# Third cross attention: five of the sixteen heads shifted by their maximum on GpSimd

## The reference

```python
scores = jnp.einsum('blhe,bshe->bhls', q, k)          # 16 heads, 77 keys
causal = jnp.triu(jnp.ones((l, s), bool), k=1)
scores = jnp.where(causal[None, None], -jnp.inf, scores)
A = jax.nn.softmax(scale * scores, axis=-1)
out = jnp.einsum('bhls,bshd->blhd', A, v).reshape(b, l, H * DV)
return out @ Wo + bo
```

## Time and profile before

| | us |
|---|---|
| median of 3 runs | 1044.64 (1040.2 to 1047.47) |
| profiled execution | 1049.98 |
| its span | 1047.8 |

### The profile page before, as it was taken

The page is one execution under the profiler, slowest core; times in us unless marked ns, Lnnn a source line. Parts: engine busy times, 40 slices in busy tenths (PEclk is TensorE's granted clock), DMA queues, the critical chain, the costliest instruction groups (busy, mean ns, idle before and its releaser), DMA issues.

```text
span 1047.8 us, 19571 instructions
## 1 busy us (share of the span) xinstructions
PE 920.8 (88%) x6337; PEld 658.4 (63%) x6337; DVE 778.0 (74%) x2080; ACT 557.4 (53%) x1494; POOL 495.5 (47%) x467
## 2 busy tenths in 40 slices
PE   6999895898778999779987698988989999989987
PEld 4787633777678999647774243434437677668873
DVE  5989998999767877779995576776734644589982
ACT  3775556896445555624442166666754233445533
POOL 5444554676066664535556667574530600024430
PEclk8999896999789999879999579999999999999998
DMA  9300000000111111500000322221002000000001
GB/s 327 150 1 1 2 6 1 1 1 1 42 39 44 40 47 32 168 1 1 0 1 30 106 59 79 60 85 47 24 18 84 1 1 1 1 2 2 1 1 40
DMA packets 29829, 40.56 MB, mean 39 GB/s; under 512 B 11468, under 2 KB 25036, under 8 KB 29228
## 3 DMA queue, kind: packets, MB, share of 16 engines
q1 hardware_dynamic: 27244, 34.28, 10.4%
q0 software_dynamic: 2496, 5.16, 1.9%
HBM read 31.44 MB, written 7.82 MB: 37 GB/s over the span
## 4 chain that ended last, share of the span: by engine, by line
PE 27%; issue 14%; POOL 8%; DVE 5%; ACT 2%; SPq 1%; DMA 0%; DVEq 0%; POOLq 0%; ACTq 0%
POOL att L1794 6%; PE ps L1169 4%; PE ps L835 4%; PE ps L825 4%; PE ps L1141 4%; PE ps L1153 3%; PE ps L799 1%; PE ps L1255 1%; PE ps L1263 1%; DVE rs L2141 1%; SPq L576 1%; PE ps L1107 1%; DVE stats L2017 0%; DVE U L2045 0%; PE ps L1112 0%
## 5 line engine op out<-in xcount | busy, mean ns | idle before, releaser
L1794 POOL TENSOR_TENSOR att<-att,ri 128x1232 f32<-128x1232 f32 x64 | 163.1, 2549 | 157.8 <-DVE ri L2147 157.8
L799 PE MATMUL ps<-VW,PT 128*128 128x128 f32 (+3 forms) x1280 | 157.6, 278 | 13.1 <-DVE x L2162 11.3
L799 PEld LDWEIGHTS ps<-VW,PT 128*128 128x128 f32 (+1 forms) x1280 | 148.4, 192 | 30.7 <-DVE x L2162 23.7
L1376 ACT ACTIVATE PT<-ps 128x512 f32<-128x512 f32 x128 | 70.5, 594 | 84.2 <-PE ps L772 83.5
L772 PE MATMUL ps<-W,att 128*128 128x128 f32 (+1 forms) x640 | 86.1, 281 | 15.1 <-POOL att L1794 13.6
L1768 POOL TENSOR_TENSOR rstd<-ve,minus_half 128x4 f32<-128x4 f32 x38 | 38.8, 1037 | 116.4 <-DVE ve L2032 99.8
L835 PEld LDWEIGHTS ps<-U,att 128*128 128x128 f32 x512 | 67.2, 194 | 33.7 <-issue 29.6
L2598 DVE CUSTOM_DVE_ANT_0 C<-ps,cmaskb 128x512 bf16<-128x512 f32 (+1 forms) x128 | 71.0, 554 | 19.6 <-PE ps L1141 16.8
L772 PEld LDWEIGHTS ps<-W,att 128*128 128x128 f32 (+1 forms) x640 | 72.0, 142 | 21.2 <-POOL att L1794 14.4
L2141 DVE TENSOR_REDUCE rs<-att 128x16 f32<-128x1232 f32 (+1 forms) x64 | 83.6, 1306 | 1.9 <-ACT att L1362 1.6
L2598 DVE CUSTOM_DVE_ANT_0 U<-ps,cmaskb 128x384 bf16<-128x384 f32 (+1 forms) x128 | 53.9, 421 | 41.6 <-PE ps L1141 41.3
(11 more groups left out here) (433 smaller groups left out, 2116.7 us busy)
## 6 DMA issues: line engine op xcount, KB each, us to landing
U<-in_ffn SPq DMA_DIRECT2D x1, 6176.0 KB, 23.0
U<-split SPq DMA_DIRECT2D x144, 32.0 KB
W<-split SPq DMA_DIRECT2D x144, 32.0 KB
W<-in_packed SPq DMA_DIRECT2D x1, 2162.5 KB, 23.9
U<-in_ffn SPq DMA_DIRECT2D x1, 2060.0 KB, 9.6
U<-in_moe SPq DMA_DIRECT2D x1, 2048.0 KB, 7.4
split<-VBD SPq DMA_DIRECT2D x4, 384.0 KB, 2.9
split<-W SPq DMA_DIRECT2D x4, 384.0 KB, 2.8
```

Source lines behind the costliest of these rows:

```text
L799: q = mm(attended(s, t), PT[0:m, t.slot(2), c, :], batch(VW, t.group)[0:m, c * D:(c + 1) * D], start=(c == 0), stop=(c == NC - 1))
L1376: go(PT[:, t.slot(2), 4 * k:4 * k + 4, :].rearrange("p c n -> p (c n)"), ps[:, k0 + k, :], ACT.Copy).then_inc(probsT, 1)
L1794: tt(p, p, over_keys(ri[:, t.slot(2), :]), ALU.mult).then_inc(probs, 1)
```

## The change

In X2, POOL subtracts the maxima of heads 0 to 4, and DVE those of heads 5 to 15. POOL's loop gets the list that it has in X1: `shift` (lag 0), then `normalize` (lag 1). `exponent` waits for `pool_shifted` as well as for `shifted`.

```diff
                     act.wait_ge(shifted, t.n + n0 + 2)
+                    if s == X2:
+                        act.wait_ge(pool_shifted, t.n + NT + 1)
...
                     pool.wait_ge(rowmax, t.n + n0 + 1)
                     a = heads(att[:, t.slot(2), :])[:, 0:BY_POOL, :]
-                    tt(a, a, over_part(mx[:, t.slot(2), 0:BY_POOL]), ALU.add).then_inc(pool_shifted, 1)
-                if s == X1:
+                    tt(a, a, over_part(mx[:, t.slot(2), 0:BY_POOL]), ALU.add if s == X1 else ALU.subtract).then_inc(pool_shifted, 1)
+                if s in (X1, X2):
                     skewed_loop(pool, [(shift, 0), (normalize, 1)], NT, TB)
...
                     elif s == X2:
-                        tt(a, a, over_keys(mx[:, t.slot(2), :]), ALU.subtract).then_inc(shifted, 1)
+                        tt(a[:, BY_POOL:H, :], a[:, BY_POOL:H, :], over_part(mx[:, t.slot(2), BY_POOL:H]), ALU.subtract)\
+                            .then_inc(shifted, 1)
```

## The result

| | before | changed |
|---|---|---|
| median, 19 runs each, us | 1046.45 | 1050.77 |
| lowest to highest | 1040.2 to 1049.54 | 1045.37 to 1054.45 |
| ratio | 1 | 1.0042, 95% interval 1.0028 to 1.0057 |

The changed kernel is slower by 4.4 us (2.9 to 6.0 by the interval), within the 1% that one would call no change, and outside chance. The forecast was 3.5 us more, 1048 in a range of 1042 to 1054. A second comparison of the same program gave 1.0028 (1.0004 to 1.0051).

A forecast was written before the change was run, and what follows sets the result against it. DVE was taken to bound X2, with PE 3% behind. Slower turns of 2.4 to 3.2 us plus 0.7 or 0.8 at the ends gave 3.5 us on a median of 1044.64, so 1048, range 1042 to 1054.

The forecast's parts named there:

- DVE as the bound before, with PE close behind: X2 before the change: DVE busy all 12 us, turn 5.78 us; PE 3% behind, about 5.61 alone.
- ceiling of a gain: X2 with DVE no longer a limit: four tiles in 22.83 us, 0.63 less, at most 2.5 us over 16 tiles.
- the rival of a gain: Both shifts in X2 run side by side, POOL's in 0.83 us; PE becomes the bound, 1042 us; chance 0.08.
- The tie of the two shifts: In X2 both shifts start at 484.92, within some hundredths; the trace can't tell which engine wins, so both worked out.
- DVE first: DVE wins the tie in X2: its shift takes 0.99, POOL's 1.68, period 5.93 instead of 5.78; 3.1 us more altogether.
- the shared time less 0.14: What an operation loses beside another engine's: POOL's shift in X2 takes 0.83 + (0.99 - 0.14) = 1.68 us.
- The new loop: X2's turn after the change: period 5.93 us, masked turn 6.3, four tiles 24.1; DVE's 0.41 becomes a wait for the exponential.
- The sum and the ends: X2: 2.4 to 3.2 us for 15 distances plus 0.7 or 0.8 at both ends; 3.5 taken.
- PE's clock falls within X2: Sign of being wrong: PE granted a lower clock in X2; no size given.
- the exponential's wait is not hidden: Denies the rival that X2's period stays 5.78 us, POOL's shift ending by 486.32; no change, 1044.6 us; chance 0.10.
- POOL never passed DVE twice: Denies the rival that POOL shifts and normalises before DVE's shift: 2.5 us per X2 tile, 40 us, 1085; chance 0.05.
- The rule of the Trainium skill: Two-input DVE and POOL operations fully block each other: X2's shifts lie end to end, 1.82 us, 1050; within small loss, 0.75.

The follow-up runs named there:

- the kernel with DVE's maximum: Changed kernel, but DVE takes maxima of heads 5 to 15 again instead of shifting them; four tiles 22.24 us, X2 100.15 us, ratio 0.9957 (0.9932 to 0.9981).

## Why the prediction was right

*DVE as the bound before, with PE close behind.* Right as to DVE. The distance of PE was read too small: I took 5.61 for PE's turn, from a turn of 5.77 less the shown wait of 0.16. It is 5.40. Without a wait a group of matmuls starts ahead of the recorded end of the one before: the transposes at 511.46, the products' end at 509.23 + 2.39 = 511.62. The idle time printed before a group counts from that end, so 0.16 of a wait isn't in it. The ceiling of a gain was thereby set at 2.5 us. The group of four in the kernel with DVE's maximum, 22.24 against 23.46, makes it (23.46 - 22.24) x 4 = 4.9. This number carried the rival of a gain and the low end of the range; the gain that it allows was 2.4 us too small.

*DVE saves 0.41 a tile.* Measured 1.399 to 0.998, 0.40.

*The tie of the two shifts.* They start within 0.01 us of each other in all 15 tiles after the first, and DVE always goes first: POOL's shift is never below 1.61 us in X2. The prediction left open who wins and worked out both; the case "DVE first" is the one that came. POOL's 1.68 is to the hundredth what was worked out from the shared time less 0.14.

*The new loop.* 5.93 forecast for a turn, 5.93 measured; 6.3 for the masked one, 6.36 measured; four tiles 24.1 forecast, 24.14 measured. The sign of what DVE does in between was right: its 0.41 turned into a wait. It shows as the end of the exponential 0.03 ahead of the sum, and as 0.26 to 0.9 of waits for PE ahead of the addition, because PE's scores come later behind the later normalisation. I had put all of it ahead of the sum, 0.55, and this wasn't there in most turns; one turn in four has a wait of 0.46 there. The addition took it up first in the others, so that wait as a sign was wrong.

*The sum and the ends.* Forecast for "DVE first" were 2.4 for 15 distances between maxima and 0.7 for the two ends (0.3 and 0.45), 3.1 in all; X2 has 3.28. From the last maximum to the last update it is 13.43 against 13.04, 0.39 more for the 0.45 forecast. From the fourth to the sixteenth maximum it is 72.39 against 70.06, 2.33 more, where twelve distances at the forecast pace make 1.9; 0.3 of the difference is one masked turn of the kernel before that took 5.84 us and not 6.14. From the first to the fourth maximum it is 19.76 against 19.20, 0.56 more, where 0.3 for the first tile and three distances make 0.8. That this part came near the forecast is luck, as the next point shows.

*The step that failed without showing in the sum* is the added wait of ACT, for which I took nothing, since ACT has 1.55 us of idle time ahead of its exponential. That holds in the loop. It doesn't hold for the first tile: the first exponential starts 6.61 us after the first addition and not 5.00, of which 0.3 are the two shifts in a row, as forecast, and 1.28 the table load. The first turn is 7.75 us instead of 6.14. The second is 6.08 instead of 5.55, for PE's scores in it take 4.47 us at the low clock. Both were paid for by the third, 5.93 instead of 7.51, in which the granted clock is full now and wasn't before: the changed kernel is granted 0.50 from 454 to 459 us, the kernel before from 458 to 460 and again from 464 to 467. PE in the third turn of the kernel before, where the changed kernel's transposes take 1.31 and its scores 2.23:

```profile
463.80 2.28 PE L772 MATMUL ps<-W,att 128*128 128x128 f32 x10 [2.42 <-POOL att L1794]
...
465.88 2.98 PE L744 MATMUL ps<-KBD,qs 128*128 x6
```

Two terms that I had not seen nearly cancel, by luck. "PE's clock falls within X2" stood among the signs of being wrong, and it does fall; but it falls in the first 20 us of the stage in the kernel before as well, so the sign tells nothing.

*From the stage to the program.* X2 explains 3.3 us. The runs say 4.4 with an interval of 2.9 to 6.0, and 2.9 the second time. I see no need for a cause outside X2, and have none. That the rest of the program keeps its times can't be told: outside X2 the two profiles of the kernel before have 944.0 and 942.8 us, those of the changed one 936.1 and 941.4, which is more spread than the effect. Of the 2.8 us between the forecast of 1048 and the median of 1050.77, 1.8 are the base: it was 1044.64 in three runs and is 1046.45 in 19. I had also expected that no difference could be told; with 19 runs of each it can, for the interval leaves out 1.

*The rivals.* The shifts don't run side by side, and the exponential's wait is not hidden. POOL never passed DVE twice; in the first tile of X2 DVE's shift waited for POOL's cast until 450.36, POOL's shift was issued at 450.33, and DVE was served first (1.62 us for DVE, 1.61 for POOL). The rule of the Trainium skill, taken alone, had POOL's shift end 1.82 us after the tie, and 1050; the rows have 1.68, so the measured share of 0.14 us decides. Its condition, two inputs in SBUF, is what the experiments bear out. The times can't tell 1048 and 1050 apart.

## What to carry to other kernels

Before work is moved from VectorE to GpSimd, look at what VectorE runs at the moment when it starts there. Here two operations that both read two inputs from SBUF didn't run side by side (1.68 us instead of 0.83), and GpSimd's price per number, 1.68 ns, then comes on top of VectorE's 1.07 on the path. An engine that is busy for all of a stage need not gain from less work when the work sits inside a loop of dependences. Put something that reads one input between (here the sum, 1.43 us), so that the meeting moves to where nobody waits, but count what the new order costs in neighbours that read each other's results (0.24 us a turn here). And where a wait is added ahead of a function on ScalarE, look whether its table load stands behind it.

## What the hardware showed that I had not expected

- Where both shifts wait for the same semaphore and are recorded as starting within 0.01 us of each other, VectorE was served first each time: in both profiles of the changed kernel in all 15 tiles after the first, and in the first one too, where it had been waiting.
- Behind a VectorE operation of 1232 numbers the next one starts 1.34 to 1.35 us later where it doesn't read that result, and 1.46 to 1.48 later where it waits for it on a semaphore.
- An added semaphore wait moved a table load of 1.28 us by 10 us, from idle time to the path.
- A kernel with a wait taken away early in a stage was slower in that stage: with the table load early, PE was granted 0.72 and 0.71 of its clock in two stretches of 6 us, one turn took 8.62 us instead of 5.93, and the clock fell again at the stage's end. That is one profile, and why the clock fell there is open.
